# One pair's scores and masks ahead of the value sums in a fused attention and mixture-of-experts block

## The reference

```python
q = jnp.einsum('bsd,hde->bhse', x, Wq)
k = jnp.einsum('bsd,hde->bhse', x, Wk)
v = jnp.einsum('bsd,hde->bhse', x, Wv)
scores = jnp.einsum('bhse,bhte->bhst', q, k)
scores = jnp.where(causal, scores / jnp.sqrt(jnp.float32(E)), jnp.float32(-jnp.inf))
attn = jax.nn.softmax(scores, axis=-1)
out = jnp.einsum('bhst,bhte->bhse', attn, v)
...
y = x + heads @ Wo
```

## Time and profile before

| what | us |
|---|---|
| median of 3 timed runs (778.43 to 781.7) | 779.05 |
| the profiled execution, its time | 777.79 |
| the profiled execution, its span | 776.0 |
| TensorE busy (share of the span) | 720.2 (93%) |
| VectorE busy | 580.1 (75%) |
| ScalarE busy | 521.5 (67%) |
| TensorE's share of the chain that ended last | 83% |

### The profile page before, as it was taken

How to read it: one execution, slowest core, us unless ns; L and a number is a source line. 1 busy time by engine, 2 the same in 40 slices (tenths; PEclk the granted TensorE clock), 3 DMA queues, 4 the chain that set the end, 5 groups by cost and what they waited for, 6 DMA issues and landing times.

```text
span 776.0 us, 17672 instructions
## 1 busy us (share of the span) xinstructions
PE 720.2 (93%) x5954; PEld 603.3 (78%) x5955; DVE 580.1 (75%) x1914; ACT 521.5 (67%) x1687; POOL 290.2 (37%) x404
## 2 busy tenths in 40 slices
PE   4999999999999999999999999999977789999954
PEld 3788878878788788878888888878767779999921
DVE  4668898989888888988889888988877444444316
ACT  4777777878777777877777777877754434444506
POOL 3024444232333423242333423241416555555525
PEclk9999999999999999999999999999979999999978
DMA  8620000000000000000000000000021132222145
GB/s 180 198 40 8 8 15 16 14 23 8 22 12 18 22 16 20 11 22 8 22 12 19 22 15 22 9 15 8 16 64 49 56 116 81 70 77 72 49 156 187
DMA packets 43701, 34.88 MB, mean 45 GB/s; under 512 B 10624, under 2 KB 40320, under 8 KB 43616
## 3 DMA queue, kind: packets, MB, share of 16 engines
q1 hardware_dynamic: 37984, 23.81, 11.4%
q0 software_dynamic: 4544, 9.45, 3.4%
q10 hardware_dynamic: 1088, 0.54, 0.2%
HBM read 20.22 MB, written 13.56 MB: 44 GB/s over the span
## 4 chain that ended last, share of the span: by engine, by line
PE 83%; DVE 4%; issue 4%; ACT 3%; POOL 2%; another core or an unknown queue 1%; DMA 1%; DVEq 1%; POOLq 0%; ACTq 0%; SPq 0%
PE PT1O L421 11%; PE M L383 9%; PE SC L404 8%; PE A L432 7%; PE A L664 7%; PE M L385 6%; PE M L384 6%; PE SC L412 4%; PE PT1O L441 4%; PE PT L446 3%; PE PT L445 3%; PE SC L407 3%; PE SC L383 2%; PE SC L385 2%; POOL expert_rows L1465 2%
## 5 line engine op out<-in xcount | busy, mean ns | idle before, releaser
L1201 ACT ACTIVATE qk<-M 128x512 f32<-128x512 f32 x127 | 76.0, 599 | 104.6 <-PE M L385 102.9
L1212 ACT ACTIVATE prob<-SC,nmax 128x256 f32<-128x256 f32 x256 | 125.4, 490 | 0.0
L1465 POOL DMA_INDIRECT expert_rows<-v_sb,got x78 | 77.4, 993 | 61.8 <-issue 31.1
L421 PE MATMUL PT1O<-pT,v_sb 128*64 128x256 f32 (+1 forms) x1024 | 98.6, 335 | 0.7 <-ACT pT L1217 0.7
L1206 ACT ACTIVATE prob<-SC,nmax 128x128 f32<-128x128 f32 x256 | 96.4, 377 | 4.3 <-DVE nmax L767 4.3
L421 PEld LDWEIGHTS PT1O<-pT,v_sb 128*64 128x64 f32 x1024 | 64.1, 138 | 42.7 <-ACT pT L1217 23.4
L775 DVE TENSOR_TENSOR prob<-prob,rden 128x512 f32<-128x512 f32 x128 | 92.5, 723 | 4.5 <-DVE rden L773 0.2
L1457 POOL DMA_INDIRECT sent_rows<-rec,slot x64 | 69.8, 1090 | 55.0 <-DVE slot L975 37.2
L767 DVE TENSOR_REDUCE nmax<-SC 128x2 f32<-128x512 f32 x128 | 87.1, 680 | 0.0
L383 PE MATMUL M<-xt_hi,wqk_hi 128*128 128x256 f32 x254 | 82.3, 324 | 4.4 <-ACT xt_st L1196 1.4
L664 PE MATMUL A<-w_sb,hidT 128*128 x624 | 78.0, 279 | 6.7 <-ACT v_sb L1335 3.3
(11 more groups left out here) (193 smaller groups left out, 1821.9 us busy)
## 6 DMA issues: line engine op xcount, KB each, us to landing
got<-sent_rows SPq DMA_DIRECT2D x39, 132.0 KB
w_in<-expert_rows SPq DMA_DIRECT2D x16, 256.0 KB, 3.5
x_in<-L_attn_x SPq DMA_DIRECT2D x16, 128.0 KB, 2.0
w_in<-L_ffn_w SPq DMA_DIRECT2D x1, 2048.0 KB, 12.1
x_res<-L_attn_x SPq DMA_DIRECT2D x16, 128.0 KB, 2.0
w_sb<-L_ffn_w SPq DMA_DIRECT2D x8, 256.0 KB, 4.7
out<-y_out SPq DMA_DIRECT2D x8, 256.0 KB, 2.1
sent_rows<-pad_rec SPq DMA_DIRECT2D x11, 132.0 KB, 4.8
```

The source lines that it names most:

```text
L421: last = mm(PT1O[k * E:(k + 1) * E, cols], v_sb[:, t, h * E:(h + 1) * E], src[:, par, k, :], start=(t == 0), stop=(t == 1), skip_group_che ...
L1212: return a.activation(prob[:, slot, k, 1:3, :].rearrange("p n t -> p (n t)"), SC[par][:, k, LATE_Q], ACT.Exp, bias=nmax[:, par, 0, k:k + 1 ...
L1465: q.indirect_dma_start(back, bass.IndirectOffsetOnAxis(ap=got[:, k, t, C_ID:C_ID + 1].bitcast(I32), axis=0), yo[:, k, t, :], None).then_in ...
```

## The change

`scores(0)` and `masks(0)` go from behind `pv_two` to ahead of it, with the two waits that stood before them. `scores(1)` and `masks(1)` stay behind it.

```diff
@@ step(b, u), TensorE
                     v_proj(turn[0], turn[1])
 
+                if more:
+                    pe.wait_ge(qk_sb, p + 4)
+                    pe.wait_ge(exp_done, p + 1)
+                    scores(0)
+                    masks(0)
+
                 if k >= 1:
                     pe.wait_ge(pt0_sb, p)
                     pe.wait_ge(pt1_sb, p)
...
                     pv_two((c - 2) % NP)
 
                 if more:
-                    pe.wait_ge(qk_sb, p + 4)
-                    pe.wait_ge(exp_done, p + 1)
-                    scores(0)
                     pe.wait_ge(exp_done, p + 2)
                     scores(1)
-                    masks(0)
                     masks(1)
```

## The result

The change makes the kernel slower. Its median is 795.63 us (793.05 to 797.15, 4 runs) against 780.38 us (778.43 to 782.3, 4 runs) for the kernel before on the same chip, a ratio of 1.0193 with a 95% interval of 1.0159 to 1.0227. The profiled execution took 794.33 us, its span 792.6; that of before 777.79 and 776.0. By the profiled executions that is +16.5 us, by the medians +15.25; the forecast was +16.

A forecast was written before the change was run, and what follows sets the result against it. TensorE's queue was taken to set the time. 60 steps x 0.32 = 19.2 us, less 3 recovered, gives +16: 777.8 + 16 = 794 us, with 788 to 801 to hold 8 in 10.

The forecast's parts named there:

- The idle time at the value sums: Before the value sums: 23.4 us blamed on ScalarE's pT copy, claimed to be tile change and not there to be won.
- The rival that the kernel gets faster: Gap at the value sums is the pT copy, the tile shape costs nothing: 768 us, chance 0.04.
- The sum of 0.32 a step: TensorE's added time per attention step, 0.10 + 0.11 - 0.10 + 0.21, bounds 0.22 and 0.44.
- masks to value sums: From SC0's masks to the first value sum, seen in no row: 0.21 taken, between 0.11 and 0.33.
- the dear switch: Rival: masks to value sums costs 0.33 in place of 0.21, 0.44 a step; +23.4, 801 us, chance 0.10.
- the cheap one: Lower bound at masks to value sums: no drain, only a mask's pitch of 0.11; 0.22 a step, 13.2 us.
- 53 ns a switch: Estimate from the skill's drain of about 128 cycles for each of two added tile switches: 6.4 us, time 781.
- 60 steps: Steps 1 to 62 without the last two pay the added time: 60 x 0.32 = 19.2 us.
- 3 us back: Recovered at 13 batches' last steps, where the projection waits for VectorE's split: 13 x 0.23, about 3 us.
- The waits at the split of x: In a batch's last step the projection starts 0.59 after the masks instead of 0.37; the added TensorE time covers this.
- The last two steps: Steps 62 and 63: added time goes into TensorE's existing waits for VectorE, 0.55 and 3.08 us, so doesn't count.
- The rival that most is taken back: No drain from masks to sums, and VectorE's earlier start relieves 6 us more projection waits: +4, 782 us, chance 0.06.

The follow-up runs named there:

- pt_first: Against the kernel before: ScalarE's pT copy moved ahead of a group of exponentials, TensorE's order unchanged; 779.31 us, ratio 0.999.
- scores_ahead_held: Against the kernel before: only SC0's scores ahead of the value sums, both masks behind SC1's scores, second half of GpSimd's scatter held back; 788.24 us, ratio 1.0103.
- masks_between: Against the kernel before: SC0's masks put between the two score blocks, all still behind the value sums; 806.61 us, ratio 1.0335.
- masks_between_held: masks_between with the second half of GpSimd's scatter issues held until TensorE finished the step's output projection; 794.85 us, ratio 1.0175 against the kernel before.
- change_held: The change with the second half of GpSimd's scatter issues held until TensorE finished the step's output projection; 793.42 us, ratio 1.0137 against the kernel before.

## Why the prediction was right

**The idle time at the value sums is a change of tile, not the pT copy.** Shown twice. The change hides the copy fully and gains nothing there; pt_first ends it 0.18 us sooner relative to the sums, and the gap stays 0.33. The rival that the kernel gets faster falls with it. Nor is it the change of PSUM bank or of number type. From masks to projection both change and the shape stays, and nothing is added: the second mask starts at 299.90 + 0.12 = 300.02, the projection's second matmul at 300.25, 0.23 for two matmuls of 0.11 to 0.12 each.

**The sum of 0.32 a step.** It came to 0.30 to 0.31, and each of its terms stands in the table above. The one that no row had shown, masks to value sums, is 0.20; I had taken 0.21 between bounds of 0.11 and 0.33. So a drain of about 0.10 stands behind a bfloat16 stream as behind the others, and neither the dear switch nor the cheap one holds. The Trainium skill's rule, in "TensorEngine Tiling (Array Packing)", section Tiling Modes, that a change of the mode drains the engine, agrees with all five places. The drain of some 128 cycles from the Trainium skill's "TensorE: Matmul & The Clock Gate", Part 2, by which the estimate was 53 ns a switch and 781 us, is too small: about 0.10 us was measured at each switch, and 795.63 us in all. That no more than the switches is at work in the step is shown by the two versions with fewer or other moves: 0.19 for one switch more (scores_ahead_held), 0.30 for two more without anything crossing the value sums (masks_between).

**60 steps, and 3 us back.** 60 x 0.305 = 18.3. The waits at the split of x are gone, 13 x 0.23 = 3.0, as the fourth steps' +0.08 and the earlier trace rows against the row of after show. The last two steps gave nothing to the end, as said: the wait of 0.55 ahead of step 62's second transposes is gone, and the one of 3.08 is 2.76 now. The rival that most is taken back falls: of the idle time put down to nobody in front of the q/k projections, 8.7 us, 6.1 are left, so what went is about the split's 3 and not the 6 more. The line of the earlier trace rows, 9.0 us, cannot be held against its 11.1 of now, since 5.0 of these stand in front of V projections, where before had 0.3.

**What the sum left out.** The late starts: in the changed kernel 0.16 in the second step of 12 batches, 1.9 us. 18.3 - 3.0 + 1.9 = 17.2, against 16.5 measured; that the forecast of 16 lies nearer is luck: its 0.32 was a little high and this term was missing. I had gone through what the move does inside a step, and not through what the added time shifts against another engine's issues: it is when the second step's transposes end that differs now against GpSimd's scatter. The timeline of all engines, second step of a middle batch of the changed kernel:

```profile
276.94 0.28 PE L385 MATMUL M<-xt_hi,wqk_lo 128*128 128x256 f32 x1
...
277.06 0.96 POOL L1460 DMA_INDIRECT sent_rows<-rec,slot  x1 [0.31 <-issue]
...
277.39 0.60 ACT L1204 ACTIVATE qk<-M 128x512 f32<-128x512 f32 x1 [0.56 <-PE M L385]
...
277.61 0.27 PE L446 MATMUL PT<-ident,prob 128*128 128x128 f32 x1
...
278.05 0.50 PE L383 MATMUL M<-wv_hi,xt_hi 128*128 128x512 f32 x1 [0.16 <-issue]
...
278.84 0.60 ACT L1220 ACTIVATE pT<-PT 128x512 f32<-128x512 f32 x1 [0.50 <-PE PT L446]
```

The projection ends at 276.94 + 0.28 = 277.22, and the q/k copy starts at 277.39, 0.17 later; so the V projection behind it starts 0.16 late. The pT copy starts at 278.84, 0.96 after the transposes' end at 277.88; masks_between pays for such a late copy. Here the moved scores and masks (1.18 us from 296.41 to 297.59 in the step shown above) stand between the V projection and the value sums and cover it. So the move does hide a late pT copy after all, but one that the kernel before does not have.

**What stays open.** That these late starts hang on the scatter is shown by the three held kernels, which change only when GpSimd issues its second half and what stands behind that in its queue. Which part of it delays the others (the issuing, its packets, or its own end) is not. An issue that lies over the transposes is not enough by itself, as the timeline of all engines of the kernel before shows at the same place:

```profile
268.26 0.96 POOL L1457 DMA_INDIRECT sent_rows<-rec,slot  x1 [0.30 <-issue]
...
268.73 0.38 PE L441 MATMUL PT1O<-ident,prob 128*128 128x128 f32 x2
...
269.15 0.42 DVE L783 COPY pT<-PT1O 128x256 f32<-128x256 f32 x1 [0.43 <-PE PT1O L441]
...
269.53 0.95 POOL L1457 DMA_INDIRECT sent_rows<-rec,slot  x1 [0.30 <-issue]
```

The third of four issues runs from 268.26 to 269.22, the transposes end in it at 269.11, and VectorE starts 0.04 later. In masks_between_held it is the third issue too (277.46), and VectorE is as prompt. In masks_between and in the change the fourth issue, 1.26 us behind the third, lies over the transposes (281.43 and 277.06), and the starts are late. In the kernel before the fourth comes only behind them, because the third comes 3.15 us after the first instead of 2.65. So it has no late starts to pay for; this is read from the traces, not tried, and why its issues are further apart is not explained.

The gap between the change and change_held, some 2 us, fits the 1.9, but the two ratios' intervals overlap, and the two profiled executions are the other way round (795.66 us held, 794.33 not). Only the intervals decide it: 9.69 for the second step, and 555.8 us from the first V projection to the last instead of 557.5.

## What to carry to other kernels

Count the changes of tile shape on TensorE before moving a block: here one switch more in a step cost 0.19 us and two more 0.30, so work of one shape is best kept together. A wait that the profile names may be covered by something that it does not name; look at what the start follows, and for a place where the named work had long been done. And a reordered step changes its phase against transfers that another engine issues, so compare the intervals of all kinds of step, not only a middle one.

## What the runs showed of the hardware that was not expected

- Where the fourth issue of GpSimd's indirect scatter (issues of 0.96 us, one each 1.26 us) lay over the transposes, an idle VectorE started 1.47 us after the matmul that it waited for had ended (masks_between), and 0.04 where the third did. With half of the scatter issued at another time, it was 0.04 again, and masks_between went from 806.61 to 794.85 us.
- The first matmul in another tile shape starts about 0.1 us late also behind a bfloat16 stream of 128x256: 0.20 after the last mask, where masks follow each other after 0.12.
- The trace goes on blaming a wait that ended 0.29 us earlier: in pt_first 21.4 us in 57 waits stand against the pT copy, 23.4 in 62 before, and ending the copy 0.18 sooner gained nothing (ratio 0.999).
